# D times the normalised rows: from a GpSimd pass in the front to a VectorE multiply in the expert tiles

## What is computed

```
xn = layernorm(x)
Bu = xn @ B_w.T                                  # 64 states
h  = causal convolution of Bu with lam ** t      # the kernel: a scan over time
y  = h @ C_w.T + D * xn
aff = (xn @ waff.T) / norms                      # 8 experts; each row goes to the best one,
keep = rank of the row within its sequence < cap #   if it is among the cap best there
moe = sum over e of keep_e * (gelu(xn @ W1[e] + b1[e]) @ W2[e] + b2[e])   # a row not kept has xn = 0 in it
out = x + y + moe
```

## Time and profile before

| | us |
|---|---|
| median of three runs | 663.0 (661.26 to 663.71) |
| the profiled execution | 663.84 |
| its span in the profile | 662.1 |
| busy PE, DVE, ACT, POOL | 589.7, 512.2, 337.3, 462.6 |

### The profile page before, as it was taken

One profiled execution on the slowest core, in us unless ns is written; L12 is line 12 of the kernel. 1 busy time (PEld: TensorE's weight loads), 2 busy tenths in 40 slices (PEclk: granted clock), 3 DMA queues, 4 the chain that ended last, 5 costly groups with the idle time before them and its releaser, 6 DMA issues.

```text
span 662.1 us, 16027 instructions
## 1 busy us (share of the span) xinstructions
PE 589.7 (89%) x4597; PEld 497.0 (75%) x4598; DVE 512.2 (77%) x974; ACT 337.3 (51%) x635; POOL 462.6 (70%) x625
## 2 busy tenths in 40 slices
PE   2988888858945599999999999999999999999994
PEld 1655555546834499898988888989898989898983
DVE  5789989799998979987667768676767676767672
ACT  5776868825799235644433435353535353535340
POOL 1999997920038838888776768787777787788453
PEclk9988868776997799999999999999999999999998
DMA  8985757611801134512212112212112212210100
GB/s 308 413 346 173 253 208 266 230 75 43 274 18 33 40 97 153 169 57 74 72 57 70 54 53 66 75 50 79 49 44 71 67 48 67 63 60 24 51 29 2
DMA packets 33584, 72.58 MB, mean 110 GB/s; under 512 B 6519, under 2 KB 19088, under 8 KB 33552
## 3 DMA queue, kind: packets, MB, share of 16 engines
q1 hardware_dynamic: 21488, 46.67, 19.7%
q0 software_dynamic: 11232, 25.20, 12.4%
q10 hardware_dynamic: 832, 0.31, 0.2%
HBM read 50.64 MB, written 27.00 MB: 117 GB/s over the span
## 4 chain that ended last, share of the span: by engine, by line
PE 69%; DVE 16%; ACT 7%; issue 6%; DMA 1%; POOL 1%; DVEq 0%; SPq 0%; ACTq 0%; POOLq 0%
PE ps_bu L820 10%; PE ps_bu L818 10%; PE ps_bu L819 10%; PE ps_t L793 5%; PE ps_y L795 5%; PE ps_t L794 5%; PE ps_y L794 5%; PE ps_t L795 5%; PE ps_y L793 5%; ACT area L494 2%; PE ps_y L662 2%; PE ps_bu L648 2%; PE ps_t L630 2%; ACT work L565 1%; PE ps_g L777 1%
## 5 line engine op out<-in xcount | busy, mean ns | idle before, releaser
L820 PE MATMUL ps_bu<-area,ring 128*128 x624 | 170.1, 273 | 1.5 <-issue 1.4
L818 PE MATMUL ps_bu<-area,ring 128*128 x624 | 170.1, 273 | 0.3
L819 PE MATMUL ps_bu<-area,ring 128*128 x624 | 170.1, 273 | 0.0
L1247 DVE SCALAR_TENSOR_TENSOR ring<-ring,h_scale 128x512 f16<-128x512 f32 x156 | 117.2, 751 | 5.6
L434 POOL DMA_INDIRECT out<-ring,idx_b x78 | 96.9, 1243 | 19.1 <-issue 14.7
L372 POOL TENSOR_TENSOR small<-ones 128x1 f32<-128x1 f32 x156 | 48.1, 308 | 86.8 <-DVE work L1161 33.4
L420 POOL DMA_INDIRECT work<-xn_rows,idx_x x78 | 87.1, 1117 | 27.1 <-issue 23.9
L444 POOL DMA_INDIRECT work<-base_rows,idx_b x78 | 92.3, 1183 | 18.0 <-issue 15.8
L596 ACT ACTIVATE ring<-ps_t,b1t,inv_in 128x256 f32<-128x256 f32 x156 | 79.2, 560 | 44.7 <-PE ps_t L795 42.4
L596 ACT ACTIVATE ring<-ps_y,b1t,inv_in 128x256 f32<-128x256 f32 x156 | 77.8, 562 | 45.9 <-PE ps_y L795 22.8
L1244 DVE TENSOR_SCALAR ring<-ring,h_scale 128x512 f16<-128x512 f32 x156 | 77.9, 499 | 23.4 <-issue 13.2
(11 more groups left out here) (267 smaller groups left out, 1085.0 us busy)
## 6 DMA issues: line engine op xcount, KB each, us to landing
ring<-L_ffn_W SPq DMA_DIRECT2D x14, 1024.0 KB, 6.4
xn_rows<-area SPq DMA_DIRECT2D x8, 1024.0 KB, 9.4
base_rows<-area SPq DMA_DIRECT2D x8, 1024.0 KB, 7.3
area<-L_attn_u SPq DMA_DIRECT2D x7, 1024.0 KB, 18.2
work<-L_ffn_W SPq DMA_DIRECT2D x5, 1024.0 KB, 9.0
work<-xn_rows,idx_x POOLq DMA_INDIRECT x78
work<-base_rows,idx_b POOLq DMA_INDIRECT x78
out<-ring,idx_b POOLq DMA_INDIRECT x78
```

The lines of the kernel that those rows point to most:

```text
L818: t.matmul(dst, hh, wh, start=(c == 0), stop=False)
L819: t.matmul(dst, hh, wl, start=False, stop=False)
L820: last = t.matmul(dst, hl, wh, start=False, stop=(c == C - 1))
L1247: v.scalar_tensor_tensor(out=hlo[p][:, cs], in0=h32[:, cs], scalar=h_scale[:, bass.ds(e, 1)], in1=hhi[p][:, cs], op0=ALU.mult, op1=ALU.sub ...
```

## The change

The product with D is no longer formed in the front. POOL has no passes there; `base_rows` now holds x + y, and `add_y` and `xn_free` do not wait for `dx_ok`. In the tiles DVE gets two instructions. `d_rows(j+1)` follows `x_low(j+1)`: one multiply of 128x512 of the gathered rows in `xg` by D, into a buffer `dx` (a ring of three; for the first two tiles the output buffer). `result(j-1)` adds that buffer to its sum before the constant row. POOL's gather for tile m waits also until `d_rows` has read the buffer that it overwrites. Because of the ring of three, DVE's loop now holds six tiles a turn and not two.

```diff
-            pool.wait_ge(s["p_late"], 4 * 16)
-            for b in range(B):
-
-                pool.wait_ge(s["xn_ok"], b + 1)
-                wait(pool, s["dx_ok"], 2 * b)
-                pieces = [slice(q * D, (q + 1) * D) for q in range(Q)]
-                for x in pieces:
-                    last = g.tensor_tensor(dxn[:, x], xn_(b)[:, x], d_bc[:], ALU.mult)
-                last.then_inc(s["dx_ok"], 1)
-                pool.wait_ge(s["dx_ok"], 2 * b + 1)
-                for x in pieces:
-                    last = g.tensor_tensor(xu_(b)[:, x], xu_(b)[:, x], dxn[:, x], ALU.add)
-                last.then_inc(s["dx_ok"], 1)
...
                     wait(pool, s["f_xt"], m - 1)
+                    wait(pool, s["dx_ok"], m - 1)
                     gate(gate_no)
...
                 dve.wait_ge(s["y_ok"], b + 1)
-                dve.wait_ge(s["dx_ok"], 2 * b + 2)
                 v.tensor_tensor(xu_(b), ps_y[:, :], xu_(b), ALU.add).then_inc(s["base_ok"], 1)
...
+            def d_rows(j, p, r, k):
+                dve.wait_ge(gx[p], k * 32 + 32)
+                dst = og[j] if isinstance(j, int) and j < 2 else dx[r]
+                v.tensor_tensor(dst.rearrange("p (h d) -> p h d", h=2), xg[p].rearrange("p (h d) -> p h d", h=2),
+                                d_bc[:, :].rearrange("p (a d) -> p a d", a=1).to_broadcast([P, 2, D]),
+                                ALU.mult).then_inc(s["dx_ok"], 1)
...
+                x_part = og[j] if isinstance(j, int) and j < 2 else dx[r]
+                dve.wait_ge(s["dx_ok"], j + 1)
+                v.tensor_tensor(yr[p], yr[p], x_part, ALU.add).then_inc(s["f_yd"], 1)
+                dve.wait_ge(s["f_yd"], j + 1)
                 v.tensor_tensor(og[p].rearrange("p (h d) -> p h d", h=2), yr[p].rearrange("p (h d) -> p h d", h=2),
...
                 x_low(j + 1, 1 - p)
+                d_rows(j + 1, 1 - p, (r + 1) % 3, k + p)
...
-            with dve.Fori(PEEL // 2, NT // 2) as i:
-                for p in range(2):
-                    step(i * 2 + p, p, i)
+            with dve.Fori(0, (NT - 1 - PEEL) // 6) as i:
+                for n in range(6):
+                    step(i * 6 + (PEEL + n), n % 2, (PEEL + n) % 3, i * 3 + (PEEL + n) // 2)
```

More of the change, by code:

```diff
@@ L31, in moe_ssm_kernel @@
     QD = Q * D
-    assert N == 64 and B * E == P and K * F == C * D and PAIRS == E and NT % 2 == 1
+    assert N == 64 and B * E == P and K * F == C * D and PAIRS == E and NT % 2 == 1 and (NT - 1 - 8) % 6 == 0
     EPS = 1e-5
@@ L135, in moe_ssm_kernel @@
         hs = [part(work, 2 * QD + n * S, S) for n in range(2)]
-        dxn = part(work, 3 * QD, QD)
         g_bc = part(work, 4 * QD, E * D)
@@ L187, in moe_ssm_kernel @@
         bg = [part(work, n * 2 * D, 2 * D) for n in range(2)]
+        dx = [part(work, at, 2 * D) for at in (3 * TE, 4 * QD + E * D + 5 * TE, 2 * TE)]
         xg = [part(work, 2 * QD + n * 2 * D, 2 * D) for n in range(2)]
@@ L220, in moe_ssm_kernel @@
             "gx0", "gx1", "gb0", "gb1", "sc0", "sc1", "ix", "ib", "gates", "cleared",
-            "f_xt", "f_xhi", "f_xlo", "f_h", "f_gelu", "f_hhi", "f_hlo", "f_y", "f_yr", "f_ym", "f_o")}
+            "f_xt", "f_xhi", "f_xlo", "f_h", "f_gelu", "f_hhi", "f_hlo", "f_y", "f_yr", "f_ym", "f_yd", "f_o")}
         def zero_out(i):
@@ L248, in xn_free @@
             eng.wait_ge(xn_out[i], 16)
-            eng.wait_ge(s["dx_ok"], 2 * (2 * i + 2))
             eng.wait_ge(s["xt_ok"], K * (2 * i + 2))
@@ L1225, in out_scales @@
                 link(v.tensor_scalar(inv_out[:, :].bitcast(I32), tmp_i[:, 0:E], 23, None, ALU.logical_shift_left))
+            gx = [s["gx0"], s["gx1"]]
             gb = [s["gb0"], s["gb1"]]
@@ L1248, in h_parts, with result @@
                                            in1=hhi[p][:, cs], op0=ALU.mult, op1=ALU.subtract).then_inc(s["f_hlo"], 1)
-            def result(j, p, k):
+            def result(j, p, r, k):
                 e = dve.value_load(tile_expert[0:1, bass.ds(j, 1)], min_val=0, max_val=E - 1)
@@ L1270, in result, with step @@
                                 ALU.add).then_inc(s["f_o"], 1)
-            def step(j, p, k):
+            def step(j, p, r, k):
                 first = isinstance(j, int) and j == 0
@@ L1288, in step @@
                 if not (isinstance(j, int) and j < 1):
-                    result(j - 1, 1 - p, k - 1 + p)
+                    result(j - 1, 1 - p, (r + 2) % 3, k - 1 + p)
             tile_scales()
             x_low(0, 0)
+            d_rows(0, 0, 0, 0)
             for n in (12, 13, 15):
@@ L1294, in _ @@
             for j in range(PEEL):
-                step(j, j % 2, j // 2)
-            with dve.Fori(PEEL // 2, NT // 2) as i:
-                for p in range(2):
-                    step(i * 2 + p, p, i)
+                step(j, j % 2, j % 3, j // 2)
+            with dve.Fori(0, (NT - 1 - PEEL) // 6) as i:
+                for n in range(6):
+                    step(i * 6 + (PEEL + n), n % 2, (PEEL + n) % 3, i * 3 + (PEEL + n) // 2)
             h_parts(NT - 1, 0)
-            result(NT - 2, 1, NT // 2 - 1)
-            result(NT - 1, 0, NT // 2)
+            result(NT - 2, 1, (NT - 2) % 3, NT // 2 - 1)
+            result(NT - 1, 0, (NT - 1) % 3, NT // 2)
 _INS = ["L0_attn_u", "L0_attn_log_lambda", "L0_attn_B_w", "L0_attn_C_w", "L0_attn_D", "L0_ffn_waff",
```

## The result

The changed kernel takes 667.8 us (median of 10 runs, 663.6 to 673.0); the kernel before, on the same chip, 663.3 (10 runs, 660.5 to 666.7). The ratio is 1.0074, 95% interval 1.0049 to 1.0099. It is slower by 4.5 us where 6.2 us faster was forecast: the prediction was wrong in sign, and the time lies above its range (652.8 to 663.5). The profiled execution has a span of 668.2 us against 662.1.

The account below looks back on a forecast made before the run. DVE, with short loops through ACT and PE, was taken to bound the front, and PE the tiles. 663.84 - 8.0 + 1.2 + 0.6 = 657.6 us, less 0.84 for the median: 656.8 us; range 652.8 to 663.5.

Parts of the forecast that it names:

- The front: Before the tiles: without POOL's passes DVE's small instructions no longer stand still, gaining 8.0 us, bounds 4 to 11.5.
- The start of the tiles: Ahead of `kept()`: two new `d_rows` instructions at 0.6 us each cost 1.2 us, bounds 0.6 to 1.9.
- The end: Last `result`, on the path, has one instruction more: cost 0.6 us.
- The tiles, as DVE's work: In the tiles: DVE's added 1.2 us a tile hides in its 1.9 us wait for PE; cost nothing, at most 2.4 us.
- POOL's new wait: In the tiles: POOL's gather starts about 5 us into the tile; base rows still arrive some 6 us early, cost nothing.
- The slower rival: In the tiles: DVE's new instructions hold POOL until it becomes the bound, 15 us more, 672 us; chance 0.10.

Follow-up runs that it names:

- e3_front_only: Kernel before without POOL's passes in the front and with no product anywhere (D times the normalised rows left out): 651.2 us, ratio 0.9859.
- e5_early4: Changed kernel with ring and loop of four; from tile 8 the product of rows j+2 is formed behind `h_parts(j)`: 655.8 us, ratio 0.9884.
- e9_early6: Changed kernel, ring of three and loop of six kept, product formed early behind `h_parts`, last six tiles written out, `result` adding rows j+3: 654.1 us.
- e2_loop2: Changed kernel with DVE's loop back at two tiles and a ring of two, `result` adding rows of two tiles later: 657.0 us, ratio 0.9931.
- e13_after_again: The changed kernel run again unaltered, on chip 4: 671.5 us, ratio 1.0106.
- e6_late4: Changed kernel with a ring of four and a loop of four tiles, the product staying where the change put it: 658.7 us, ratio 0.9944.
- e12_no_base: `e4_phase` without the gathers of base rows, DVE adding the zeros in the buffers instead: 661.2 us, one execution, no gap.
- e14_pool20: `e4_phase` with POOL's steps 8 to 19 written out instead of looped: 696.9 us, one execution, 87 gaps.
- e15_pool_flat: Changed kernel with all of POOL's steps written out, no hardware loop on POOL: 655.2 us, ratio 0.9863.
- e7_phase2: Kernel before, DVE's loop of two tiles, with POOL also waiting from tile 3 for `f_xlo` of two tiles back: 666.1 us, ratio 1.0052.
- e8_phase6: Kernel before with POOL also waiting for `f_xlo` of two tiles back, and DVE's loop of six tiles: 666.9 us, ratio 1.007.
- e4_phase: Kernel before with one more POOL wait: from tile 3 its step for tile m waits for DVE's first low part (`f_hlo`) of tile m-3: 688.5 us.
- e10_pe20: `e4_phase` with PE's tiles 8 to 19 written out instead of looped: 725.7 us, one execution, 118 gaps.
- e17_base_from_xn: `e4_phase` with the third pair of gathers reading `xn_dram` in place of `base_dram`: 662.8 us, one execution, no gap.
- three experiments here: `e4_phase` with base gathers reading `xn_dram`, without scatters except the last two tiles, or with base gathers ahead of scatters: 662.8, 662.9 and 661.6 us.

## Why the prediction was wrong, point by point

**The front: right, and a little too careful.** The eight profiles without POOL's passes have the reciprocal at 128.4 to 133.5 us, mean 130.9; the twelve with them at 138.4 to 142.4, mean 140.0. The gain is 9.1 us over all and 6.6 in the one pair of profiles; forecast 8.0, bounds 4 to 11.5. How near these come to 8.0 is partly chance: single profiles of one kernel differ by up to 1.8 us in this mark (130.7 and 132.5 for the changed one). `e3_front_only`, with nothing put in the tiles, is 1.4% faster than the kernel before; its median is 10.7 us lower on one chip, some of it from a lower excess (1.9 for 4.3 us). DVE's excess in the small instructions is gone, and a part of it came back as the longer waits above.

**The start of the tiles: slightly dearer.** 1.85 us in the first pair, inside the bounds; over all kernels with the product, from the reciprocal to tile 2, 101.9 to 103.1 us against 100.6 to 101.3 without. Forecast 1.2, bounds 0.6 to 1.9. L1227 takes 0.68 us and its successor starts 0.60 behind it, as costed.

**The end: right**, +0.7 for 0.6.

**The tiles, as DVE's work: right.** With the early place, the two instructions a tile leave an excess of 0.5 and 1.2 us (`e5_early4`, `e9_early6`), no more than the kernels without them. They are hidden in DVE's wait for PE.

**POOL's new wait, "Cost nothing in one step": this is the step that failed**, by +10.1 us in the profiled pair. Its facts held. POOL's step does start late, its index copy 5.4 us into the tile where little is disturbed (`e2_loop2`) and 6.3 in the changed kernel, and the base rows are in time. What failed is the conclusion that a step which is in time costs nothing wherever it lies. I asked only whether somebody would wait for its data, not what its transfers would run beside once moved by 5 us. What the runs show in its place: beside POOL's transfers PE's counts come late, by up to 3.9 us in the changed kernel, ACT and DVE start late by as much, and PE loses time in gaps. The kernel before already showed this, in 16 gaps of "issue" on PE, 15 of them within 4.1 us behind a gather of base rows, and in this row of its waits (328 to 594 us), and I used neither:

```profile
ACT ring L596 <- remote: 10.3, 6, 3.2
```

The slower rival was the right sign with the wrong mechanism: POOL keeps its wait for DVE, and DVE holds it no more than before. POOL's transfer instructions take 1.24, 1.15 and 1.08 us on average (scatter, base rows, xn) against 1.27, 1.16 and 1.08.

**What stays open.** Shown by undoing it: the late place costs 17 us in the changed kernel (`e13_after_again` against `e9_early6`, which differ also in the written-out last six tiles and in which rows are added) and 3 us with the ring of four (`e6_late4` against `e5_early4`, which differ in nothing else). The gathers of base rows take part (`e12_no_base` against `e14_pool20`, one chip, one execution each). Not shown is by what means POOL's transfers make PE's counts late, nor why PE stands. Nor is it shown why the late place is nearly harmless in `e2_loop2`, `e6_late4` and `e15_pool_flat`. They differ from the changed kernel in the code of a loop, but that changed nothing where the place alone was shifted (`e7_phase2` and `e8_phase6`). They also ran on chips 12, 15 and 2, where the changed kernel never ran. The chip is thus a rival that no run excludes: on chip 4 even the kernel before had executions up to 669.4 us, for 666.7 at most elsewhere. A late place makes the gaps possible; how many come I can't predict. The median start of the first base gather, 2.1 us in the changed kernel, 3.1 in `e4_phase` and 2.9 in `e10_pe20`, is partly an effect of the gaps, since they push POOL on: it is 1.4 us in `e17_base_from_xn`, with the wait of `e4_phase` and no gap.

**The better version.** `e5_early4` leaves nothing out and is 1.2% faster than the kernel before, as `e15_pool_flat` is by 1.4%. The change is worth making if the product is formed behind `h_parts`. Both edits together weren't tried.

## What to carry to other kernels

A wait that moves another engine's step is not free because its data still arrive in time: ask what the moved transfers now run beside. Before counting on a full engine, look for idle time put down to "issue" on it and to "remote" on the engines that wait for it, and for where both stand relative to those transfers. Compare an experiment only with a kernel that ran on the same chip: without it three experiments here say nothing. When an engine that others wait for needs the new result, form it in the place where it already waits for the bound, one step ahead, so that it releases its buffer at the old time. A time lost in a stretch that was costed at nothing is best found by putting the same work into both places.

## What the runs showed of the hardware that I had not expected

Beside indirect DMAs issued by POOL the semaphore counts of PE, and of PE alone, can come late: by up to 3.9 us in the changed kernel and 5.1 us in `e14_pool20`, while no count of ACT, DVE or POOL was late by more than 0.013 us. ACT and DVE then wait, although PE's instruction ended long ago by its row. At times PE stops too, in gaps of 0.2 to 0.74 us in the changed kernel, which within a train follow one another at about 0.75 us, with no semaphore and no instruction fetch to show for it. In the worst kernel they stretched the median tile from 10.92 to 12.9 us. On one chip, in three kernels with the same kind of transfers, none of this appeared: 35 tiles in a row took 10.92 us each, and no count was more than 0.015 us late.
